# An attention and feed-forward layer on eight cores: the transposes and the small matmul of each feed-forward chunk are put behind the next chunk's projection

## The reference, cut to what matters

```python
def _L0_ffn_ref(x, U, V, W1, b1, W2, b2):
    h = jax.nn.relu(jnp.einsum('bsd,de->bse', x, W1) + b1)
    alpha = jax.nn.softmax(jnp.einsum('bse,ek->bsk', h, W2) + b2, axis=-1)
    vx = jnp.einsum('krd,bsd->bskr', V, x)
    uvx = jnp.einsum('kdr,bskr->bskd', U, vx)
    out = jnp.einsum('bsk,bskd->bsd', alpha, uvx)
    return out

x = _layernorm(x + attn(x, ...))
x = _layernorm(x + _L0_ffn_ref(x, U, V, W1, b1, W2, b2))
```

## Time and profile before

| | |
|---|---|
| median of 10 runs | 2014.36 us (2011.01 to 2077.48) |
| the profiled execution | 2011.05 us, with a span of 2009.4 us on the slowest core, core 0 |
| spans of the eight cores | 1997.1 to 2009.4 us |
| TensorE (PE) busy | 1327.7 us, 66% of the span |
| weight loads of TensorE (PEld) | 652.5 us, 32% |
| DVE, ACT, POOL busy | 26%, 20%, 11% |
| granted TensorE clock, mean of core 0 | 0.761 of full speed |

### The profile page before, as it was taken

The page is one execution under the profiler, slowest core; times in us unless marked ns, Lnnn a source line. Parts: engine busy times, 40 slices in busy tenths (PEclk is TensorE's granted clock), DMA queues, the critical chain, the costliest instruction groups (busy, mean ns, idle before and its releaser), DMA issues.

```text
span 2009.4 us, 18600 instructions; the slowest of 8 cores (1997.1 to 2009.4 us)
## 1 busy us (share of the span) xinstructions
PE 1327.7 (66%) x6704; PEld 652.5 (32%) x6800; DVE 532.4 (26%) x886; ACT 408.7 (20%) x552; POOL 221.6 (11%) x208
## 2 busy tenths in 40 slices
PE   2358988869975556786665547977554678665552
PEld 1124444434433333342322223423333334232220
DVE  2013233330012223444310352001222344431035
ACT  0000000001134444211100131113444431110013
POOL 2000000000011111420100001001111143100000
PEclk6669999979975556898677768977555589877776
DMA  9940100016040001769705529944100167960402
GB/s 175 173 76 21 43 22 23 20 63 105 0 70 16 1 1 26 107 127 220 129 10 75 74 63 212 167 71 62 23 1 1 21 105 134 203 105 14 71 0 83
DMA packets 61322, 146.24 MB, mean 73 GB/s; under 512 B 7344, under 2 KB 11824, under 8 KB 55856
## 3 DMA queue, kind: packets, MB, share of 16 engines
q0 software_dynamic: 54608, 102.90, 33.4%
q1 hardware_dynamic: 5472, 33.76, 5.1%
q10 hardware_dynamic: 1152, 8.39, 1.1%
HBM read 237.45 MB, written 8.39 MB: 122 GB/s over the span
## 4 chain that ended last, share of the span: by engine, by line
PE 47%; DMA 15%; DVE 14%; ACT 9%; issue 7%; POOL 4%; another core or an unknown queue 2%; DVEq 1%; ACTq 0%; POOLq 0%
PE fb L245 45%; DMA wob<-wo 4%; DMA wkb<-wk 4%; DMA w1b<-w 3%; PE tb L245 2%; DMA wvb<-wv 2%; POOL wbf L265 2%; ACT rbuf L265 1%; DVE x1bufs L265 1%; DVE scrf L265 1%; DVE msq L265 1%; ACT wrw L265 1%; ACT cfm L265 1%; DMA w2b<-w 1%
## 5 line engine op out<-in xcount | busy, mean ns | idle before, releaser
L245 PE MATMUL fb<-w1b,x2fm 128*128 128x512 bf16 x496 | 146.2, 462 | 41.0 <-DMA w1b<-w 37.8
L245 PE MATMUL fb<-wvb,xpf 128*128 128x512 bf16 x503 | 119.4, 397 | 33.6 <-DMA wvb<-wv 33.0
L245 PE MATMUL fb<-wob,ofm 128*128 128x512 bf16 x500 | 118.1, 397 | 20.9 <-DMA wob<-wo 19.7
L245 PE MATMUL fb<-wgb,xmf 128*128 128x512 bf16 x500 | 125.0, 412 | 4.5 <-DVE psf L265 3.6
L245 PE MATMUL fb<-wvb,xmf 128*128 128x512 bf16 x502 | 117.6, 395 | 13.7 <-DMA wvb<-wv 13.0
L245 PEld LDWEIGHTS fb<-w1b,x2fm 128*128 128x128 bf16 x512 | 57.5, 115 | 123.7 <-issue 88.8
L265 DVE TENSOR_TENSOR okb<-fb,rbuf 128x256 f32<-128x256 f32 x32 | 13.6, 425 | 310.9 <-ACT rbuf L265 168.4
L245 PE MATMUL tb<-idb,scrb 128*128 128x128 bf16 x256 | 29.5, 280 | 96.8 <-ACT scrb L265 56.9
L245 PE MATMUL fb<-wsb,xpf 128*128 128x512 bf16 x249 | 67.6, 435 | 37.4 <-DMA wsb<-ws 23.2
L245 PEld LDWEIGHTS fb<-wvb,xpf 128*128 128x128 bf16 x512 | 51.3, 101 | 99.0 <-issue 44.7
L245 PEld LDWEIGHTS fb<-wob,ofm 128*128 128x128 bf16 x512 | 51.7, 102 | 86.9 <-issue 32.2
(11 more groups left out here) (149 smaller groups left out, 1896.9 us busy)
## 6 DMA issues: line engine op xcount, KB each, us to landing
strip<-x_main SPq DMA_DIRECT2D x24, 1024.0 KB, 10.1
wgb<-wg POOLq DMA_DIRECT2D x16, 1024.0 KB, 20.3
wob<-wo POOLq DMA_DIRECT2D x16, 1024.0 KB, 22.9
w1b<-w POOLq DMA_DIRECT2D x16, 1024.0 KB, 24.4
wsb<-ws POOLq DMA_DIRECT2D x8, 1024.0 KB, 25.5
strip<-x_pre SPq DMA_DIRECT2D x8, 1024.0 KB, 7.2
wkb<-wk POOLq DMA_DIRECT2D x8, 1024.0 KB, 40.1
wvb<-wv POOLq DMA_DIRECT2D x4, 2048.0 KB, 71.6
```

Source lines behind the costliest of these rows:

```text
L245: t.matmul(o, l, r, start=a, stop=b, is_transpose=(True if tpp else None)))
```

## The change

T(c) and M(c) move into a function `ts_mal`. It is not called in chunk c; a closure is kept in `ts_pend[0]` and called in the next pass of the loop, after G(c+1) (and, for `wh` = 0, VX(c+1) with its `vxsb` copy) and ahead of h(c+1). The last chunk of `wh` = 0 is so carried over into the first chunk of `wh` = 1, behind G'(0), and the last chunk of `wh` = 1 is called after both loops. No instruction is added or removed.

```diff
+            ts_pend = [None]
+
+            def ts_mal(c, wh, hr):
+                nonlocal mal, scrb_free
+                HC2 = D2 // 128
+                tts = []
+                for k0 in range(0, HC2, 4):
...
+                        mt = mm(bnk[0:128, j * 128:(j + 1) * 128],
+                                scrb.ap(0, 128, (k0 + j) * 128, 128),
...
+                                waits=[hr, t_idb, bfree(bnk)] if j == 0 else (),
+                                inc=(j == nk - 1), tp=True)
+                    evt = vop(lambda v, b=bnk, nk=nk, k0=k0: v.tensor_copy(
+                        hfm.ap(0, 128, k0 * 128, nk * 128),
+                        b[0:128, 0:nk * 128]), waits=[mt] + hfm.birth)
...
+                    scrb_free = P.cur("MM")
+                for k2 in range(HC2):
...
+                    mal = mm(FB[5][0:128, c * KE:(c + 1) * KE],
...
+                             waits=([tW2(-1), bfree(FB[5])] + tts) if first
+                             else tts,
+                             inc=lastg)
+
             for wh in range(2):
                 tw12 = (tw12_0 if wh == 0 else
                         load_w_into(w1buf, w1, D, D, col0=D2, ncols=D2,
...
                         bset(FB[4], vxe)
+                    if ts_pend[0] is not None:
+                        ts_pend[0]()
+                        ts_pend[0] = None
                     ha = None
...
                     scrf_free = hr
-                    tts = []
-                    for k0 in range(0, HC2, 4):
...
-                bWo = phase_barrier()
+                    ts_pend[0] = (lambda c=c, wh=wh, hr=hr: ts_mal(c, wh, hr))
+            ts_pend[0]()
+            ts_pend[0] = None
+            bWo = phase_barrier()
             AR.freebuf(w1buf, toks=phase_barrier())
```

More of the change, by code:

```diff
@@ L1331, in build_program @@
             vxwb_free = None
+            ts_pend = [None]
[4 more added lines that the diff above has]
+                for k0 in range(0, HC2, 4):
+                    nk = min(4, HC2 - k0)
+                    bnk = TBK[k0 // 4 % 2]
+                    mt = None
+                    for j in range(nk):
+                        mt = mm(bnk[0:128, j * 128:(j + 1) * 128],
+                                scrb.ap(0, 128, (k0 + j) * 128, 128),
+                                idb_sb.h[0:128, 0:128],
+                                start=(j == 0), stop=(j == nk - 1),
+                                waits=[hr, t_idb, bfree(bnk)] if j == 0 else (),
[3 more added lines that the diff above has]
+                        b[0:128, 0:nk * 128]), waits=[mt] + hfm.birth)
+                    bset(bnk, evt)
+                    tts.append(evt)
+                    scrb_free = P.cur("MM")
+                for k2 in range(HC2):
+                    first = (wh == 0 and c == 0 and k2 == 0)
+                    lastg = (wh == 1 and c == NHC - 1 and k2 == HC2 - 1)
+                    mal = mm(FB[5][0:128, c * KE:(c + 1) * KE],
+                             hfm.ap(0, 128, k2 * 128, 128),
+                             w2b.ap(0, 128, (wh * HC2 + k2) * KE, KE),
+                             start=first, stop=lastg,
+                             waits=([tW2(-1), bfree(FB[5])] + tts) if first
+                             else tts,
+                             inc=lastg)
             for wh in range(2):
```

## The result

The changed kernel takes 1931.64 us (median of 9 runs) against 2013.75 us before (32 runs). The ratio is 0.959, with a 95% interval of 0.9573 to 0.9608: 4.1% faster. The prediction was 1935 us with a range of 1927 to 1959.

The account below looks back on a forecast made before the run. TensorE, busiest yet idle about a third of the span, bounds through its waits. Savings of 39.5 (20.4 + 4.4 + 14.7) and 40.0 us, together 79.5, give 1931.6, or 1935 us on the median's scale; range 1927 to 1959.

Parts of the forecast that it names:

- h(c) lies in the open and goes under G(c+1): Feed-forward loop: TensorE idles for h(c), 3.96 us; after the change it runs under G(c+1), 6.91 us.
- The boundary that is left, 2.42 us in wh = 0 and 1.69 in wh = 1: TensorE stop per chunk boundary after the change, M waiting for DVE copies; some 6 and 5 us before.
- the 1.85 of the sum: TensorE from T to the next G in wh = 1: 0.56 to first copy, 0.95 copies, 0.15 and 0.19.
- The load comes earlier by what is saved ahead of it: Second load of W1: issue 4.7 us after VX(3) starts instead of 9.09; 4.4 us saved a half, besides wh = 0.
- The time from issue to the end of G'(0), taken as unchanged: Second load of W1: an earlier issue meets the same empty queues, so G'(0) moves along with it.
- wh = 1 saves 14.7 and 15.4 us: End of G'(0) to end of M'(3): 47.40 us becomes 32.7 in the first half; the second saves 15.4.
- The clock holds over the boundary: TensorE keeps full clock behind the shorter boundaries, with 1.5 or 1.05 us idle; chance 0.75, 1935 us.
- My bound of 20 us: Gain in G(2), G(3) and three G' that hangs on the clock: 9.9 us a half, 20 us in all.
- The Trainium skill's rule on transposes: At the boundaries: transposes do not count as TensorE work for the full clock; the sum would lose 20 us.
- Idle throughout: What a boundary would be for the clock if transposes do not count; the sum would lose 20 us.
- The rest moves along: Softmax, utb stage and the next half's loads, issued from the loop's end or later, all move up with it.
- The signs named: Marks of being right, first half: second w1b issue near 1024, M'(3) ending near 1089, boundaries of 2.4 and 1.7 us.

Follow-up runs that it names:

- the kernel with the load at G(3): Changed kernel, but the second load of W1 waits for G(3) alone and not for T(2): 1923.97 us, ratio 0.9549.
- the slow copy: Changed kernel with one more DVE reduction of some 2.4 us ahead of the second copy of each T: 1979.86 us, ratio 0.9827.
- the parts wh = 0 and wh = 1: Kernel before, with the deferral kept for wh = 0 only: 1974.46 us, ratio 0.9804; for wh = 1 only: 1988.00 us, ratio 0.982.

## Why the prediction was right, step by step

- **h(c) lies in the open and goes under G(c+1).** Shown: T has no idle time before it but in the drains, 5.0 us in all, and the relu's wait in the kernel before could be filled with matmuls that cost no time.
- **The boundary that is left, 2.42 us in wh = 0 and 1.69 in wh = 1.** Shown: TensorE goes from T to G in 2.44 us, and VX(0) to VX(3) is 35.94 us for the forecast 35.9. In wh = 1 T to G is 1062.92 - 1061.06 = 1.86 (the 1.85 of the sum). That the `vxsb` copy is 0.57 us of the first is shown by its change of place (1.62 us idle before M, then 1.05).
- **The load comes earlier by what is saved ahead of it.** Shown: VX(3) to issue 4.67 us for the forecast 4.7, and the kernel with the load at G(3) gained the 8 us that an issue 3.9 us earlier gives in two halves. The time from issue to the end of G'(0), taken as unchanged, was off by -1.2 and +2.4 us on these two cores. Over eight cores and both halves it is 31.05 us on average before and 31.00 after, and spreads from 28.3 to 32.3 and from 27.9 to 33.8: the assumption holds for the average, and the two halves differ by less than 1 us. That the queues were empty rests on more than the earlier trace rows, which end at 1006.40: the DMA share of the kernel before is 0.00 from there to 1049.74.
- **wh = 1 saves 14.7 and 15.4 us.** It saved 14.5 and 13.4. The second half's G'(1) took 8.95 us, not 7.07: its last piece of G'(0) ran at the 1.2 GHz level (3.57 us for 8) and the clock had not come back. In the first half G'(1) had the full clock behind the same row. So the clock behind G'(0) was the one place where "held" was too simple, at 1.9 us; over the eight cores it was lost there in 4 of 16 halves.
- **The clock holds over the boundary.** Shown, with a reversal in both directions: filling the stop gives the clock back in the kernel before, and 2.39 us more idle time takes it away in the changed one. My bound of 20 us for it fits: 48 us were lost with the slow copy (49.8 in the loops), 14 x 2.39 = 33 of them as idle time, so some 15 are left for the clock.
- **The Trainium skill's rule on transposes.** The Trainium skill ("TensorE: Matmul & The Clock Gate", Part 4: PE-mode transpose) would have had the clock fall. It did not here: with bf16 transposes in the wait, G stayed at 7.07 us where it was 8.64 us with the wait empty. The measurement decides against the rule for this kernel. ("Idle throughout", as I put it, was 0.35 us too much in any case: M's eight matmuls are no transposes.)
- **The rest moves along.** Shown by the sum: 76.1 us on the two profiled cores, 76.8 us between their spans. The forecast of 79.5 was 3.4 too high there, by the load of the second half (2.4) and the G'(1) behind it (1.9), less the 1.2 that the first half's load was quicker; the median moved by 82 us, and so hides that. Against the 77.6 us of all eight cores the forecast is 1.9 us too high, most of it in wh = 1 (14.4 us a half for 14.7 and 15.4). The signs named came out: the issue at 1021.76 for "near 1024" and the end of M'(3) at 1085.11 for 1089, with VX(0) itself 2.6 us earlier than before.

What stays open is small: why the time from the issue of the load to the end of G'(0) spreads over 6 us from core to core, and why the part of the kernel outside the loops differs by some 5 us between executions. By whole times alone it would also be open whether the parts wh = 0 and wh = 1 add up to the whole (39 and 36 us against 82, each with an interval of some 13 us either way); the loops have them at 41.0 and 32.5 against 77.6.

## What to carry to other kernels

When engines work fixed lists, put a chain over three engines behind the next block of independent work on the engine that bounds, and then look at what stands ahead of each link on the other engines: the wait that is left is there (here 1.62 us, of which a copy in the way makes 0.57). Price a stop of TensorE with the clock behind it, not only with its own length: here 2.4 us of a G of 9.3. A wait written as "all work issued so far" changes its meaning when work is moved or added; tie it to the instruction that matters.

## What the runs showed of the hardware

The kernel before got faster by 232 matmuls whose results nobody uses, by 26.8 us in its loops and 36 us (25 to 46) by its times, because they ran where TensorE had been idle and kept it at the 2.4 GHz level. And transposes in bf16 keep that level too: a wait of the same length cost G its clock when it was empty (8.64 us) and not when 46 transposes stood in it (7.07 us).
